# First expert layer: tokens routed chunk by chunk into regions of one expert each, first tiles with resident weights, 15 further tiles by table, results gathered by token

## The reference, cut to what matters

```python
h = _layernorm(x, axis=-1) * (1 + ca) + sa
x = x + ga * _L0_attn_ref(h, ...)          # recurrence over 1024 tokens, 2 batches
h = _layernorm(x, axis=-1) * (1 + cb) + sb
x = x + gb * _L0_ffn_ref(h, ...)
...
def _L0_ffn_ref(h, router_w, w1, b1, w2, b2):
    x = h.reshape(-1, d)                    # 2048 tokens, d = 128
    logits = x @ router_w                   # 16 experts
    assign = jnp.argmax(logits, axis=-1)
    w = jax.nn.sigmoid(jnp.take_along_axis(logits, assign[:, None], axis=1)[:, 0])
    hh = jax.nn.gelu(jnp.einsum('nd,edf->nef', x, w1) + b1, approximate=False)   # f = 256
    all_out = jnp.einsum('nef,efd->ned', hh, w2) + b2
    out = jnp.take_along_axis(all_out, assign[:, None, None], axis=1)[:, 0, :]
    return (out * w[:, None]).reshape(b, s, d)
```

## Time and profile before

| | us |
|---|---|
| median of 3 runs | 738.57 (735.44 to 739.32) |
| profiled execution, its own time | 738.83 |
| its span in the profile | 737.0 |

### The profile page before, as it was taken

How to read it: one execution, slowest core, us unless ns; L and a number is a source line. 1 busy time by engine, 2 the same in 40 slices (tenths; PEclk the granted TensorE clock), 3 DMA queues, 4 the chain that set the end, 5 groups by cost and what they waited for, 6 DMA issues and landing times.

```text
span 737.0 us, 26362 instructions
## 1 busy us (share of the span) xinstructions
PE 652.8 (89%) x10871; PEld 551.6 (75%) x10871; DVE 432.6 (59%) x1365; ACT 290.0 (39%) x964; POOL 277.5 (38%) x422
## 2 busy tenths in 40 slices
PE   5898888888820998799999999999999899999996
PEld 4565655666710987588888888888887799898996
DVE  3768888877150332356777777686767555444443
ACT  1434444442110431354555545454544343333322
POOL 2435555544235575001323324232423343232216
PEclk9679999989755999699999999999999999999999
DMA  7980000000215693000000000000040365666562
GB/s 223 306 192 3 2 2 2 3 2 3 115 27 174 200 311 94 1 4 4 4 11 11 15 11 12 15 8 15 8 151 10 100 209 209 222 214 221 200 206 80
DMA packets 46086, 66.31 MB, mean 90 GB/s; under 512 B 5632, under 2 KB 34912, under 8 KB 43024
## 3 DMA queue, kind: packets, MB, share of 16 engines
q1 hardware_dynamic: 40080, 56.79, 24.3%
q0 software_dynamic: 3424, 7.08, 2.7%
q10 hardware_dynamic: 2464, 0.76, 0.4%
HBM read 49.92 MB, written 19.02 MB: 94 GB/s over the span
## 4 chain that ended last, share of the span: by engine, by line
PE 54%; DVE 2%; DMA 2%; issue 1%; ACT 0%; POOL 0%; SPq 0%; DVEq 0%; POOLq 0%
PE bank L1742 6%; PE quad L1600 6%; PE quad L1724 5%; PE quad L1726 5%; PE bank L1625 4%; PE pair L1562 3%; PE bank L1649 3%; PE quad L1606 2%; PE pair L1563 2%; PE bank L1662 2%; PE pair L1564 2%; PE bank L1665 2%; PE pair L1587 2%; PE bank L1652 2%; DMA f_xg<-moe_slots 2%; PE bank L1744 1%
## 5 line engine op out<-in xcount | busy, mean ns | idle before, releaser
L2000 DVE TENSOR_TENSOR h_masked<-quad,const 128x1536 f32<-128x1536 f32 (+2 forms) x66 | 112.5, 1705 | 57.1 <-PE quad L1606 47.9
L1836 ACT ACTIVATE f_sa<-quad 128x256 f32<-128x256 f32 (+1 forms) x115 | 40.1, 351 | 93.8 <-PE quad L1726 76.2
L2114 DVE TENSOR_TENSOR f_hid<-f_sa,quad 128x256 f32<-128x256 f32 (+1 forms) x115 | 43.0, 379 | 53.1 <-ACT f_sa L1836 53.0
L1724 PE MATMUL quad<-f_xT,f_w 128*128 128x256 f32 (+1 forms) x190 | 51.0, 350 | 2.8 <-DVE f_hid L2114 2.7
L1742 PE MATMUL bank<-f_w,f_hid 128*128 128x128 f32 x390 | 50.7, 277 | 1.1 <-DVE f_hid L2117 0.9
L1742 PEld LDWEIGHTS bank<-f_w,f_hid 128*128 128x128 f32 x390 | 47.8, 192 | 3.6 <-DVE f_hid L2117 2.8
L1726 PE MATMUL quad<-f_xT,f_w 128*128 128x256 f32 (+1 forms) x190 | 49.7, 343 | 0.0
L2223 POOL DMA_INDIRECT moe_slots<-g_pay,g_slot x28 | 28.5, 1019 | 54.4 <-DVE g_pay L1968 43.4
L1600 PE MATMUL quad<-h_qk 32*128 32x128 f32 x1024 | 47.0, 298 | 0.0
L1813 ACT ACTIVATE h_gT<-bank 128x128 f32<-128x128 f32 x64 | 17.7, 277 | 63.4 <-PE bank L1652 63.4
L1600 PEld LDWEIGHTS quad<-h_qk 32*128 32x128 f32 x1024 | 34.7, 187 | 10.2 <-issue 8.4
(11 more groups left out here) (375 smaller groups left out, 1820.3 us busy)
## 6 DMA issues: line engine op xcount, KB each, us to landing
f_w<-moe_w SPq DMA_DIRECT2D x23, 1088.0 KB, 5.2
e_w<-in_experts_dram SPq DMA_DIRECT2D x32, 257.5 KB, 4.9
moe_slots<-blank SPq DMA_DIRECT2D x2, 2112.0 KB, 15.5
moe_slots<-zero SPq DMA_DIRECT2D x4, 516.0 KB, 4.0
e_xg<-moe_slots SPq DMA_DIRECT2D x8, 258.0 KB, 3.1
f_xg<-moe_slots SPq DMA_DIRECT2D x12, 132.0 KB, 4.2
moe_w<-in_moe_w_dram SPq DMA_DIRECT2D x1, 1408.0 KB, 7.2
moe_w<-in_moe_w_dram SPq DMA_DIRECT2D x1, 1280.0 KB, 10.5
```

The costliest lines, as they stand in the source:

```text
L1724: pe.matmul(up_bank(n, f)[:, 0:s], w[:, F1 + TAIL1 + f * P:F1 + TAIL1 + (f + 1) * P], x_of(n)[:, 0:s], start=True, stop=True)
L1836: act.activation(sa[g % 3][:, 0:s], up_bank(n, f)[:, 0:s], ACT.Silu).then_inc(f_sa, 1)
L2000: dve.tensor_tensor(masked[k % 4][:, :, a * P:z * P], quad[:, :, a * P:z * P], cst("causal")[:, None, a * P:z * P].to_broadcast([P, HPG, ( ...
L2114: dve.tensor_tensor(hid[n % 2][:, f, 0:s], sa[g % 3][:, 0:s], up_bank(n, f)[:, T1:T1 + s], ALU.mult)\
```

## The change

The routing moves into the recurrence. In step i (from 2 on) and in the drain, chunk i - 2 is routed: PE `transpose_h`, `logits`, `ranks`, ACT `take_h`, DVE `choose` and `place_of`, POOL `send`, which also counts the tokens of each expert so far (`cum`). Each expert gets a region of 2048 rows (`REGION`) in DRAM, so a token's slot needs no total counts: it is the region's start plus its rank. The regions (17.8 MB) are filled with zeros in four groups (`SLABS`), by as many rows as the chunks so far can need; rows carry no token number any more. All 16 experts' weights are loaded into SBUF (`wall`) during the recurrence. In the expert phase the first tile of each region is processed by fixed addresses, then 15 further tiles (`EXTRA0`) by a table of expert and row. Each result is stored over its tile's rows, and POOL gathers the results by the slots kept in `slot0`: chunk 0 at the end of the phase, the others in layer two. The last step leaves out the last state update. Buffers of layer two lie in `wall` and `h_all`.

```diff
+REGION = BATCH * SEQ
+SLOTS = E0 * REGION + (EXTRA0 + 1) * P
+SLABS = ((0,), (1, 2), (3, 4), (5, 6, 7))
...
+            for g, slabs in enumerate(SLABS):
+                for s in slabs:
+                    for k in range(2):
+                        sp.dma_start(regions[s, k], blank[:, 0:1, 0:C].to_broadcast([P, E0, C])).then_inc(s_slab[g], 16)
+                if g == 1:
+                    sp.dma_start(wall[:, :, :], t["experts0"].rearrange("e p n -> p e n")).then_inc(s_wall, 16)
...
+            def choose(n):
+                dve.wait_ge(s_rlog, n + 1)
+                for b in range(BATCH):
+                    dve.max(mx_bc[:, b, n, :], logit[:, b, :]).then_inc(s_rmx, 1)
+                for b in range(BATCH):
+                    dve.wait_ge(s_rmx, n * BATCH + b + 1)
+                    dve.max_index(idx[:, b, :], mx_bc[:, b, n, :], logit[:, b, :]).then_inc(s_ridx, 1)
...
+            def send(n):
+                pool.wait_ge(s_place, n * 2 + 2)
+                pool.tensor_copy(slot_bc[:, :, n], place[:, :]).then_inc(s_slot, 1)
+                count(n)
+                for g, slabs in enumerate(SLABS):
+                    if slabs[0] == n:
+                        pool.wait_ge(s_slab[g], 16 * (2 * len(slabs) + (g == len(SLABS) - 1)))
+                pool.wait_ge(s_slot, n + 1)
+                for b in range(BATCH):
+                    c = b * CHUNKS + n
+                    pool.indirect_dma_start(out=t["moe0_slots"], out_offset=bass.IndirectOffsetOnAxis(
+                        ap=slot[:, c:c + 1], axis=0), in_=h_all[:, c, :], in_offset=None).then_inc(s_sent, 16)
...
@@ POOL, step
                 if prepare:
                     mix(i + 1)
+                if i >= 2:
+                    send(i - 2)
                 if tail:
                     moe_deviation(i - 1, 1 - q)
...
@@ SP, expert phase
+            def load_weights(d):
+                e = sp.value_load(expert[0:1, d:d + 1], min_val=0, max_val=E0 - 1)
+                if d >= RING:
+                    sp.wait_ge(e_y, E0 + d - RING + 1)
+                sp.dma_start(wdyn[d % RING][:, :], t["experts0"][bass.ds(e, 1), :, :].rearrange("e p n -> p (e n)"))\
+                    .then_inc(s_wt[d % RING], 16)
...
+            def store_extra(d):
+                r = row_of(d)
+                sp.wait_ge(e_y, E0 + d + 1)
+                sp.dma_start(t["moe0_slots"][bass.ds(r, P), :], yg[:, d, :]).then_inc(s_outd, 16)
...
+            for d in range(EXTRA0):
+                store_extra(d)
+                if d + RING < EXTRA0:
+                    load_weights(d + RING)
...
@@ PE, expert phase
+            for _ in range(12):
+                pe.matmul(bank[5][:, 0:2 * P], cst("ident"), const[:, 0:2 * P], start=True, stop=True)
+            for n in range(-2, ALL + 3):
+                if n + 2 < ALL:
+                    transpose(n + 2)
+                if 0 <= n < ALL:
+                    up(n)
+                if n >= 3:
+                    down_product(n - 3)
...
+def gather_results(pool, t, yt, slot, c, s_back):
+    for b in range(BATCH):
+        n = b * CHUNKS + c
+        pool.indirect_dma_start(out=yt[:, n, :], out_offset=None, in_=t["moe0_slots"],
+                                in_offset=bass.IndirectOffsetOnAxis(ap=slot[:, n:n + 1], axis=0)).then_inc(s_back[c], 16)
```

538 lines of the change are left out of this document (276 added, 262 removed).

## The result

The changed kernel takes 747.98 us (median of 12 runs, 740.67 to 753.44) against 736.23 us before (12 runs of the same series, 731.67 to 741.09). The ratio is 1.012, 95% interval 1.0087 to 1.0152: slower, by 1.2%, where I had forecast 721.7 us and given faster 0.88. The profiled execution took 748.2 us with a span of 746.3, so its span can be set against the 737.0 of before.

The account below looks back on a forecast made before the run. The recurrence was taken as a chain around DVE, the expert phase as set by SP's queue, layer two as PE-bound. 738.83 - 28.4 + 11.5 = 721.9, less 0.26 to the median: 721.7 us, own range 714 to 732, with rivals 707 to 736.

Parts of the forecast that it names:

- What bounds the kernel: Whole kernel: recurrence step a chain around DVE, expert tiles and layer two PE-bound, 55 of 100.3 us no expert work.
- PE's transposes replace filler: Recurrence steps with routing: PE's transposes take the place of filler products, so they add no time.
- PE's clock falls more often: Rival, recurrence: less filler, PE idles more, three more steps at the lower level, 2.7 us each; 730 us, chance 0.10.
- The routing itself, 2.15 us a step: Steps 2 to 6: 1.3 us for DVE and rank products plus 0.85 for POOL's late deviation, 10.8 for five steps.
- The fills costed at nothing: Recurrence: 17.8 MB of fills and 4.2 MB of weights add no time, the queue being empty from 50 us on.
- the rival that ended slower by starving: Rival, recurrence: sends wait for slow fills; at 128 GB/s POOL and the state stand 21 us; 743 us, chance 0.06.
- Scatters stall behind DVE: Rival, recurrence: each scatter held for one DVE instruction, send 5.8 us, recurrence +14.6; 736 us, chance 0.08.
- From the last token on, 71.9 us: Last normalised token to layer two: 8.6 + 4.3 + 53.3 + 5.7 us against 100.3 before, a gain of 28.4.
- SP's queue sets the end, not PE: Expert phase: 45 pairs of register load and transfer, 1.14 us apart, plus stores, 53.3 us; PE would need 42.
- Gathers at nothing: Layer two: seven pairs of gathers, 2.3 us each, hidden in POOL's idle time, so no cost.
- The stretch to the last token: Recurrence with routing: +11.5 us, from 10.8 for five steps, +0.3 in step 7 and +0.4 in the drain.
- The upper bounds of a step: Recurrence step: at most 2.7 us later with nothing of DVE and ranks hidden, and 2 for POOL's late deviation.

Follow-up runs that it names:

- e11: The kernel before, without routing in the recurrence, with filler at step starts and behind level one left out from step 2 on: 777.0 us, ratio 1.027.
- e1: The changed kernel with the filler products put back at step starts and behind the logits in steps that have a routing: 730.2 us, ratio 0.989.
- e12: The changed kernel with filler back, extra tiles' weights requested by POOL, region fills spread over steps, layer two's slot fills requested first: 740.5 us, ratio 0.979.
- e4: The changed kernel with the 15 loads of extra tiles' weights requested by POOL instead of SP: 743.0 us, ratio 1.003.
- e5: The changed kernel with both the filler of e1 and the weights requested by POOL of e4: 723.8 us, ratio 0.982.

## Why the prediction was wrong, point by point

- **What bounds the kernel.** Right for the expert layer. For the recurrence I wrote that part of PE's 160 busy us "is filler" and that the step is a chain around DVE. Both are true, and the conclusion drawn from them, that filler may be traded for work, was the mistake.
- **"PE's transposes replace filler", costed at nothing.** This is the step that failed. 0.38 and 0.62 us of routing in the places of 1.03 and 1.13 us of filler left PE idle for 1 us twice, and PE at its lower level for part of every step: 3.3 us in step 4, where the sum had 0. The rows behind it were in the trace of before: the filler and the gaps beside it, 0.38 and 0.47 us. Put back, the filler is worth 13.7 us in the six steps (144.1 to 130.4), 17.8 us between the medians.
- **The rival "PE's clock falls more often".** The right mechanism, with its sign, and mis-sized twice. I counted three more such steps; it is all five that lost filler (0.66 to 0.72), and step 1 (0.78) by the stop. And I priced one at 2.7 us from the earlier trace rows, where PE fell near the step's end; with the fall at its start the difference is 3.3 (23.42 for 20.09 us) to 4.7 (25.21 for 20.55), and 5.0 to 5.4 in the two steps of e11 at a clock of 0.65. Against it I had held that the routing products take the fillers' places: they are shorter than what they replace.
- **The routing itself, 2.15 us a step.** Right, when the clock is at its upper level. Steps 3 to 6 of e1 are 1.3 to 1.8 us longer than those of before at full clock. Steps 2 to 6 of e12 sum to 103.9 us; five at the 18.94 that steps 2 to 5 of before take on average are 94.7: +9.2, a stop of 1.45 us in step 4 included, where I had 10.8.
- **The fills costed at nothing.** I asked only whether they are fast enough, and they are: no send waited for a fill. The changed kernel's last fill is done near 117 us, at about 345 GB/s in the 16 pieces of 512 bytes that lie 1 MiB apart, above the 256 of the earlier trace rows. So the rival that ended slower by starving falls. The Trainium skill (DMA: Bandwidth & Descriptors, Latency and other measured facts) gives 207 GB/s at a row pitch of 512 KiB and 164 at 2 MiB, for copies between HBM tensors with that pitch from partition to partition; here the 1 MiB lies between the pieces of one partition, and the trace shows no such loss. What the fills and the load of weights did cost, most likely through the fetch of PE's instructions, is 7.7 us of the six steps (130.4 in e1, 122.7 in e12): stops, and the lower clock behind them, in a form that I had not on the list. By what stood beside the stops the load of all weights and the fills of layer two's slots count for more than the fills of the regions; no run leaves one of them out. Of this nothing was in the trace of before, where the transfers were over when the steps began.
- **"Scatters stall behind DVE".** Refuted: 0.96 to 1.23 us in the steps, for 0.95 to 1.24 before. The 3.1 us that the Trainium skill (SBUF — State Buffer, A bandwidth-pool intuition that's wrong) gives for a POOL transfer beside a DVE copy show nowhere: in step 4 a scatter of 1.10 us starts at 138.81, within DVE's copies of 138.57 to 139.57.
- **From the last token on, 71.9 us.** Measured 76.1. By its terms: SP's pairs 53.0 us (238.54 to 291.56) for 53.3; table 5.0 for 4.3; end 6.5 for 5.7; and the first 11.5 for 8.6, since between the last scatter (issued until 230.28) and SP's first load (233.50) lie 3.2 us for its landing and the new block, where I had 1.2. "SP's queue sets the end, not PE" holds, by e4 and e5, but PE stood only 7.5 us behind it.
- **Gathers at nothing.** They take 0.95 to 1.09 us, and layer two's chunks start 33.4 us apart as before.
- **The two misses together.** The stretch to the last token is 19.2 us above its forecast (30.7 for 11.5). The filler accounts for 13.7 and the stops for 7.7, less 1.6 by which the routing was cheaper than its sum: 19.8, close to the whole.
- **Slips in the sums.** The send was added up with a gap of 0.2 us where the text and the earlier trace rows have 0.3. The upper bounds of a step, 2.7 and 2, make +24 us for the recurrence and not +22, so the forecast's own range ends at 734. "Faster" adds up to 0.87, not 0.88. None of them changes the outcome.

## What to carry to other kernels

Filler on TensorE is a load-bearing part: when work takes its place, compare their busy times and the idle gaps at that place, and put back the difference; gaps of 1 us where there were 0.4 cost 3.3 to 4.7 us a step here. Where a kernel's own transfers fill the DMA engines beside a long unrolled program, look at the instruction queue's packets and at idle time "issue" on PE, spread the transfers, and look first at the largest: fills of 1 MB, one or two at a time, stood beside no stop above 0.2 us here. Whether the load of 4.1 MB in pieces would end the last stop was not tried. An expected gain on one stretch is only half of a prediction; the stretch that pays must be priced with its clock, not at the full one.
